# Maxima of a head group: one long spreading copy by ScalarE, or a short one and a spread by VectorE

## The chip, the cores and the metric
The kernel runs on one core of a Trainium2 chip. The metric is the device time of one execution in microseconds (us), as the median of several runs. The engines are TensorE (PE, its weight loads PEld), VectorE (DVE), ScalarE (ACT), GpSimd (POOL) and SyncE (SP, which issues the DMAs). Each runs its own instructions in order, and they wait for one another by semaphores.

## The reference, cut to what matters
Two layers, each a gated attention and a gated block of attention with a mixture of experts, over 16 sequences of 256 tokens with 256 channels, 16 heads of 16 channels:

```
x = x + tanh(g_xattn[0]) * xattn0(ctx, layernorm(x), ...)     # stage 0: keys and values from ctx, key bias and mask
x = x + tanh(g_ffn[0])   * ffn0(layernorm(x), ...)            # stage 1: self attention + top-2 of 8 linear experts
x = x + tanh(g_xattn[1]) * xattn1(layernorm(x), ctx, ...)     # stage 2: 512 keys, half of them from ctx
x = x + tanh(g_ffn[1])   * ffn1(layernorm(x), ...)            # stage 3: causal attention, then top-2 of 8 GELU experts
attn = softmax(q k^T + bias);  out = attn v                   # in each stage, for each head
```

What matters here is the softmax: for each query and head the maximum of its 256 (in stage 2, 512) scores is subtracted before the exponential.

## The kernel before, in words
The attention part takes the four stages u = 0 to 3 one after another, and in each the 16 sequences b; a pair (u, b) is a job. In a job each head h goes through these steps:

- `S`: TensorE multiplies queries by keys into one of two PSUM banks `s_ps` (L870 to L876). VectorE takes the row maxima into `mx` (L1112; in stage 3 with the causal mask, L1105) and gives the bank back (`s_read`).
- `M`: once for each group of HG = 8 heads (two groups a job), GpSimd negates the 8 maxima of every query and splits each into three bf16 parts (L1043 to L1050), in `mp` [128 queries, 27 columns] for each half of the tokens: 3 columns of ones and 3 x 8 parts.
- `MT`: TensorE transposes `mp` into rows 96 to 122 of `tr_ps` (L883), 27 rows of 256 queries. ScalarE copies these rows into rows 96 to 122 of `qs`, the stacked query operand, once for each of the 8 heads of the group: one ACTIVATE whose input is read 8 times (L989). It gives `tr_ps` back (`tr_read`).
- `T`: TensorE multiplies keys by queries, transposed, into one of two banks `t_ps`; the 27 extra rows of `ks` and `qs` add the bias and subtract the maximum (L901, in stage 3 L897 and L898). The first T of a group waits for MT's copy. ScalarE takes the exponential into `ex` (L995) and gives the bank back (`t_read`). In stage 3 GpSimd clears the future keys (L1035).
- `PV`: after four heads TensorE multiplies by the values (L926) and ScalarE copies the result out (`ot`, L999). `OT`: TensorE transposes it into `tr_ps` (L937), the same bank that MT uses, and VectorE divides by the sums (L1119, L1121) and gives the bank back, also by `tr_read`.

Around them are layer norms (`LNS`, `LNP`, `LNX`; L1077, L1014, L1090), projections `Q`, `K`, `V`, `PROJ`, their split into bf16 parts on GpSimd (L1026 to L1030), DMAs that stack the parts as rows, in stage 1 the experts (L847, L1176), and `FIN` (L1197) or `PROJ`, which end a job.

The order of the instructions on each engine is not written by hand. `orders()` is a planner that runs when the kernel is built: a list scheduler over all steps of all jobs, with a cost in microseconds for each step and engine (`STAGES`), a hop between engines (`HOPS`), and the rules of the banks. Each engine then issues its instructions in the order found, and the `*_AT` tables turn the order into semaphore counts. So a changed cost in `STAGES` can move any step in any queue of the attention part.

```
"M": [("pool", 1.3)], "MT": [("pe", 0.12), ("act", 1.86)],
act.wait_ge(tr_ready, TR_AT[step] + 1)
act.activation(qs[q_at][PRODUCTS:ROWS, k * HG:(k + 1) * HG, :],
               tr_b[PRODUCTS:ROWS, 0:T].unsqueeze(1).broadcast_to([ROWS - PRODUCTS, HG, T]), ACT.Copy).then_inc(tr_read, 1)
```

Behind the attention part (from about 1920 us) come routing, the experts of the last stage and their combination, each a part of its own.

Of the kernel before, what the change touches and what calls it, by code (L numbers as in the profile page):

```python
# [7 lines left out]
BF16 = mybir.dt.bfloat16  # L8
# [3 lines left out]
ACT = mybir.ActivationFunctionType  # L12
# [3 lines left out]
B, T, D = 16, 256, 256  # L16
# [13 lines left out]
HG = H // G  # L30
# [8 lines left out]
PRODUCTS = 6 * HD  # L39
# [21 lines left out]
def kv_at(u, b, src=0):  # L61
# [14 lines left out]
    "UNBIAS": [("dve", 1.8)], "BPROJ": [("pool", 1.27)],  # L76
    "GATE": [("pe", 0.9), ("dve", 0.65)], "GEXP": [("act", 0.22)], "TOP": [("dve", 0.6)],
# [3 lines left out]
    "OTT": [("pe", 0.44), ("act", 0.6)], "PROJ": [("pe", 0.87), ("pe", 0.87), ("dve", 0.75)], "FIN": [("dve", 0.86)],  # L81
    "STOREX": [("sp", 0.5), ("wire", 7.5)]}
# [228 lines left out]
def counted(steps):  # L311
    return {s: n for n, s in enumerate(steps)}


def of_kind(engine, *names):
    return [s for s in dict.fromkeys(ORDER[engine]) if s[0] in names]
# [9 lines left out]
TR_AT = counted(of_kind("pe", "MT", "OT"))  # L326
PRE_AT = counted(of_kind("pe", *PRE))
M_AT = counted(of_kind("pool", "M"))
KSPLIT_AT = counted(of_kind("pool", "KSPLIT"))
QSPLIT_AT = counted(of_kind("pool", "QSPLIT"))  # L330
VC_AT = counted(of_kind("pool", "VC"))
# [141 lines left out]
def attention_phase(nc, a):  # L473
# [3 lines left out]
    with own:  # L477
# [20 lines left out]
        qs = ring("qs", NQ, [ROWS, H, T], BF16); ks = ring("ks", NKV, [ROWS, H, T], BF16)  # L498
        va = ring("va", NKV, [P, NT, H, VW])
        mx = ring("mx", NQ, [P, H, 2])  # L500
        mr = ring("mr", 2, [P, NT, HG]); mp = ring("mp", 4, [P, NT, ROWS - PRODUCTS], BF16)
        ex = sb("ex", [P, EXPS, 2 * T])
        ot = ring("ot", 2, [P, T])
# [29 lines left out]
        xn_ready, vc_ready, bproj_added, moments, rooted = sem("xn_ready"), sem("vc_ready"), sem("bproj_added"), sem("moments"), sem("rooted")  # L533
        s_ready, s_read, t_ready, t_read = sem("s_ready"), sem("s_read"), sem("t_ready"), sem("t_read")
        m_ready, tr_ready, tr_read, pv_ready, pv_read = sem("m_ready"), sem("tr_ready"), sem("tr_read"), sem("pv_ready"), sem("pv_read")
        past_kept = sem("past_kept")
        lg_ready, lg_exp, top_done, fin_done = sem("lg_ready"), sem("lg_exp"), sem("top_done"), sem("fin_done")
        dve_step, pool_step = sem("dve_step"), sem("pool_step")

# [139 lines left out]
        with nc.Block() as block:  # L679
# [93 lines left out]
            def _(pe):  # L773
# [29 lines left out]
                for step in ORDER["pe"]:  # L803
# [74 lines left out]
                    elif name == "MT":  # L878
                        pe.wait_ge(m_ready, M_AT[("M", u, b, k)] + 1)
                        if TR_AT[step]:  # L880
                            pe.wait_ge(tr_read, TR_AT[step])
                        for t in range(NT):
                            last = pe.transpose(tr_b[PRODUCTS:ROWS, t * P:(t + 1) * P], mp[(2 * j + k) % 4][:, t, :], ident_b[:, :])  # L883
                        last.then_inc(tr_ready, 1)
                    elif name == "T":
                        n = T_AT[step]
                        h, src = k
                        if step == T_FIRST[(u, b, h // HG)]:
                            pe.wait_ge(tr_read, TR_AT[("MT", u, b, h // HG)] + 1)
                        if n >= 2:  # L890
                            pe.wait_ge(t_read, n - 1)
                        at = kv_at(u, b, src)
                        if u == 1 and b < NKV and step == T_FIRST[(u, b, h // HG)]:
                            pe.wait_ge(bias_set, UNBIAS_AT[("UNBIAS", u, b, 0)] + 2)
                        dst, key = t_ps[n % 2], ks[at % NKV]
                        if u == 3:
                            pe.matmul(dst[:, 0:T], key[0:ROWS, h, 0:P], qs[q_at][0:ROWS, h, :], start=True, stop=True)  # L897
                            last = pe.matmul(dst[:, T:T + P], key[0:ROWS, h, P:T], qs[q_at][0:ROWS, h, P:T], start=True, stop=True)  # L898
                        else:
                            for t in range(NT):  # L900
                                last = pe.matmul(dst[:, t * T:(t + 1) * T], key[0:ROWS, h, t * P:(t + 1) * P],  # L901
                                                 qs[q_at][0:ROWS, h, :], start=True, stop=True)
                        last.then_inc(t_ready, 1)
                    elif name == "PV":
                        v = PV_AT[step]
                        srcs = sources(u)
                        slots = {(i, r): T_AT[("T", u, b, (k * QH + i, r))] for i in range(QH) for r in range(srcs)}
                        if u == 3:
                            pe.wait_ge(past_kept, max(PAST_AT[("T", u, b, (k * QH + i, 0))] for i in range(QH)) + 1)
                        else:  # L910
                            pe.wait_ge(t_read, max(slots.values()) + 1)
                        if u == 0:
                            pe.wait_ge(vc_ready, VC_AT[("VC", u, b, 0)] + 1)
                        else:
                            wait_copied(pe, ("V", u, b, 0))
                        if u == 2:
                            pe.wait_ge(vc_loaded[b % 2], 16 * (b // 2 + 1))
                        if v:
                            pe.wait_ge(pv_read, v)
                        for r in range(srcs) if turns(step) == 1 else (turn,):  # L920
                            val = va[kv_at(u, b, r) % NKV]
                            for t in range(NT):
                                q0 = P if u == 3 and t == 1 else 0
                                for i in range(QH):
                                    e = ex[:, slots[(i, r)] % EXPS, t * T:t * T + T - q0]
                                    last = pe.matmul(pv_ps[i * VW:(i + 1) * VW, q0:T], val[:, t, k * QH + i, :], e,  # L926
                                                     start=r == 0 and t == 0, stop=r == srcs - 1 and t == NT - 1,
                                                     tile_position=(0, i * VW))
                        if ends:
                            last.then_inc(pv_ready, 1)  # L930
                    elif name == "OT":
                        v = PV_AT[("PV", u, b, k)]
                        pe.wait_ge(pv_read, v + 1)
                        if TR_AT[step]:
                            pe.wait_ge(tr_read, TR_AT[step])
                        for t in range(NT):
                            last = pe.transpose(tr_ps[:, t * P:(t + 1) * P], ot[v % 2][:, t * P:(t + 1) * P], ident[:, :])  # L937
                        last.then_inc(tr_ready, 1)

            @block.scalar  # L940
            def _(act):
                for step in ORDER["act"]:
# [35 lines left out]
                    elif name == "V":  # L978
                        wait_values_free(act, u, b, sources(u) - 1)
                        dst = va[kv_at(u, b, sources(u) - 1) % NKV]  # L980
                        end_pre(act.activation(dst[:, :, :, 0:HD], bank[:, :].rearrange("p (t h d) -> p t h d", t=NT, h=H), ACT.Copy))
                    elif name == "CT":
                        end_pre(act.activation(combt[j % 2][:, :], bank[0:E, 0:T], ACT.Copy))
                    elif name == "GEXP":
                        act.wait_ge(lg_ready, LG_AT[("GATE", u, b, 0)] + 1)
                        act.activation(flat(pr[j % 2]), flat(lg[j % 2]), ACT.Exp).then_inc(lg_exp, 1)
                    elif name == "MT":
                        act.wait_ge(tr_ready, TR_AT[step] + 1)
                        act.activation(qs[q_at][PRODUCTS:ROWS, k * HG:(k + 1) * HG, :],  # L989
                                       tr_b[PRODUCTS:ROWS, 0:T].unsqueeze(1).broadcast_to([ROWS - PRODUCTS, HG, T]), ACT.Copy).then_inc(tr_read, 1)  # L990
                    elif name == "T":
                        n = T_AT[step]
                        act.wait_ge(t_ready, n + 1)
                        w = 3 * P if u == 3 else 2 * T
                        act.activation(ex[:, n % EXPS, 0:w], t_ps[n % 2][:, 0:w], ACT.Exp).then_inc(t_read, 1)  # L995
                    elif name == "PV":
                        v = PV_AT[step]
                        act.wait_ge(pv_ready, v + 1)
                        act.activation(ot[v % 2][:, :], pv_ps[:, 0:T], ACT.Copy).then_inc(pv_read, 1)  # L999
# [56 lines left out]
            def _(dve):  # L1056
# [7 lines left out]
                for step in ORDER["dve"]:  # L1064
# [33 lines left out]
                    elif name == "S":  # L1098
# [11 lines left out]
                        else:  # L1110
                            dst = mx[q_at][:, h, src:src + 1] if u == 2 else mx[q_at][:, h, :]
                            dve.tensor_reduce(dst, s_ps[n % S_BANKS][:, :].rearrange("p (a b) -> p a b", a=dst.shape[-1]), AX.X, ALU.max).then_inc(s_read, 1)  # L1112
                    elif name == "OT":
                        v = PV_AT[("PV", u, b, k)]
                        dve.wait_ge(tr_ready, TR_AT[step] + 1)
# [745 lines left out]
```

## Time and profile before

| | us |
|---|---|
| three runs | 2731.59, 2734.83, 2737.47 (median 2734.83) |
| the profiled run | 2733.68 |
| its span from first to last instruction | 2732.0 |
| TensorE busy in the span | 2326.2 (85%) |
| VectorE | 1705.4 (62%) |
| ScalarE | 1381.1 (51%) |
| GpSimd | 917.7 (34%) |

A row of a group of instructions reads: line, engine, operation, output <- input by the program's names, out <- in (partitions x elements, type), xcount | busy us, mean ns of one | idle time of the engine just before them, and what ended it. Matmuls are pipelined and their ends are modelled, so a busy TensorE isn't one at its peak. Waits name who came last.

### The profile page before, as it was taken

The page shows a single profiled execution, that of the slowest core. Times are in us where ns is not written, and L with a number is a line of the kernel's source. Part 1 is how long each engine was busy: PE and PEld are TensorE (multiplying, and loading weights), DVE is VectorE, ACT ScalarE, POOL GpSimd, SP SyncE. Part 2 cuts the span into 40 slices and gives each one's busy share as a digit, 9 for nine tenths or more (in the row PEclk, how much of TensorE's full clock was granted, in tenths as well). Part 3 has the DMA queues.
Part 4 walks back from the last instruction along what each step waited for, and adds up shares of the span by engine and source line. Part 5 has one row for each costly group of instructions (what it writes and reads, how often), then busy time and mean ns, then how long its engine had stood idle before and what let it go on. Part 6 is the DMA issues. An engine that isn't in the chain of part 4 may idle for free. (4 is left out here: it accounts for less than half of the span.)

```text
span 2732.0 us, 52598 instructions
## 1 busy us (share of the span) xinstructions
PE 2326.2 (85%) x17492; PEld 1615.3 (59%) x17493; DVE 1705.4 (62%) x4564; ACT 1381.1 (51%) x2430; POOL 917.7 (34%) x1769
## 2 busy tenths in 40 slices
PE   3889899999999999999999999898337999999920
PEld 1445555455555555666566666665337999999920
DVE  4668796766776766766766667665455434344358
ACT  3779863454444447777777777676110222222211
POOL 5355322131232152233322257665001333333321
PEclk9989999999999999999999999999556999999965
DMA  7888633242332354454454446553560111111144
GB/s 227 215 210 209 150 97 78 51 96 55 81 82 76 94 126 117 118 122 117 113 126 118 104 110 140 133 129 76 204 189 12 35 36 36 35 35 34 36 148 167
DMA packets 214243, 296.34 MB, mean 108 GB/s; under 512 B 33109, under 2 KB 152703, under 8 KB 207776
## 3 DMA queue, kind: packets, MB, share of 16 engines
q1 hardware_dynamic: 183808, 253.78, 36.5%
q10 hardware_dynamic: 23328, 22.06, 2.6%
q0 software_dynamic: 6912, 17.97, 2.1%
q8 instruction: 115, 1.88, 0.3%
q14 instruction: 80, 0.66, 0.1%
HBM read 201.41 MB, written 93.22 MB: 108 GB/s over the span
## 5 line engine op out<-in xcount | busy, mean ns | idle before, releaser
L1112 DVE TENSOR_REDUCE mx<-s_ps 128x2 f32<-128x512 f32 (+1 forms) x1024 | 657.2, 683 | 217.5 <-PE s_ps L870 141.3
L995 ACT ACTIVATE ex<-t_ps 128x512 f32<-128x512 f32 (+1 forms) x1280 | 683.8, 577 | 191.7 <-PE t_ps L901 146.9
L901 PE MATMUL t_ps<-qs,ks 123*128 123x256 bf16 x2048 | 362.1, 278 | 10.3 <-ACT ex L995 6.5
L926 PE MATMUL pv_ps<-ex,va 128*32 128x256 f32 (+1 forms) x5120 | 324.7, 380 | 2.5 <-POOL ex L1035 2.5
L989 ACT ACTIVATE qs<-tr_ps 27x2048 bf16<-27x2048 bf16 x128 | 239.4, 1870 | 146.5 <-PE tr_ps L883 143.8
L847 PE MATMUL pre_ps<-wexp,xt 128*128 128x512 f32 x512 | 264.5, 625 | 6.8 <-DVE moe L1176 2.6
L1631 PEld LDWEIGHTS x_up_ps<-x_rows_t,x_wnow 128*128 128x128 f32 x2272 | 266.4, 193 | 5.3 <-issue 0.9
L1631 PE MATMUL x_up_ps<-x_rows_t,x_wnow 128*128 128x128 f32 x2272 | 267.0, 276 | 1.1 <-DVE x_pre L1694 0.7
L901 PEld LDWEIGHTS t_ps<-qs,ks 123*128 123x128 bf16 x2048 | 175.0, 99 | 143.4 <-ACT ex L995 66.2
L1641 PE MATMUL x_y_ps<-wdn,x_act 128*128 x1136 | 257.1, 379 | 0.7 <-DVE x_y L1702 0.7
L1661 ACT ACTIVATE x_rows_t<-x_rt_ps 128x256 f32<-128x256 f32 x72 | 27.7, 384 | 439.8 <-PE x_rt_ps L1620 439.8
L1641 PEld LDWEIGHTS x_y_ps<-wdn,x_act 128*128 128x128 f32 x1136 | 210.3, 190 | 26.8 <-issue 1.1
L876 PE MATMUL s_ps<-ks,qs 99*128 99x256 bf16 (+1 forms) x1024 | 190.3, 286 | 36.5 <-DVE mx L1112 25.1
L926 PEld LDWEIGHTS pv_ps<-ex,va 128*32 128x32 f32 x5120 | 142.2, 111 | 131.6 <-issue 49.9
L1105 DVE CUSTOM_DVE_ANT_0 s_ps<-s_ps,late 128x128 f32<-128x128 f32 (+1 forms) x512 | 166.6, 388 | 64.1 <-PE s_ps L873 63.7
L1043 POOL TENSOR_SCALAR mp<-mx 128x16 bf16<-128x16 f32 x128 | 34.8, 272 | 505.2 <-DVE mx L1112 473.6
L870 PE MATMUL s_ps<-ks,qs 96*128 96x256 bf16 x1024 | 185.1, 275 | 21.3 <-DVE mx L1112 16.0
L1689 DVE COPY x_wnow<-wup 128x1024 f32 x144 | 98.8, 688 | 141.8 <-PE x_up_ps L1631 135.4
L876 PEld LDWEIGHTS s_ps<-ks,qs 99*128 99x128 bf16 (+1 forms) x1024 | 89.0, 101 | 139.3 <-DVE mx L1112 75.2
L999 ACT ACTIVATE ot<-pv_ps 128x256 f32<-128x256 f32 x256 | 99.0, 387 | 142.6 <-PE pv_ps L926 140.1
L1176 DVE SCALAR_TENSOR_TENSOR moe<-pre_ps,comb,moe 128x256 f32<-128x256 f32 x256 | 123.1, 481 | 61.6 <-PE pre_ps L847 55.3
L1026 POOL TENSOR_TENSOR ak<-ak,pk 128x512 f32<-128x512 f32 x64 | 74.1, 1158 | 232.5 <-ACT pk L976 135.3
(254 smaller groups left out, 3764.1 us busy)
## 6 DMA issues: line engine op xcount, KB each, us to landing
q_parts<-pq SPq DMA_DIRECT2D x128, 192.0 KB
qs<-q_parts SPq DMA_DIRECT2D x64, 384.0 KB, 5.0
qs<-q_parts SPq DMA_DIRECT2D x192, 128.0 KB, 5.8
k_parts<-pk SPq DMA_DIRECT2D x96, 192.0 KB
ks<-k_parts SPq DMA_DIRECT2D x96, 192.0 KB
ks<-k_parts SPq DMA_DIRECT2D x288, 64.0 KB
ks<-ctx_k_parts SPq DMA_DIRECT2D x64, 192.0 KB
ks<-ctx_k_parts SPq DMA_DIRECT2D x192, 64.0 KB
```

The costliest lines, as they stand in the source:

```text
L847: end_pre(step, pe.matmul(bank[:, :], xt_now[:, turn, t * P:(t + 1) * P], wexp[:, turn, e:e + 2, :].rearrange("p e n -> p (e n)"), start=t ...
L870: last = pe.matmul(dst[:, r * T:(r + 1) * T], q(src), key(r)[0:rows, h, :], start=True, stop=True)
L876: last = pe.matmul(dst[:, t * T:(t + 1) * T], q(t), key(0)[0:rows, h, :], start=True, stop=True)
L901: last = pe.matmul(dst[:, t * T:(t + 1) * T], key[0:ROWS, h, t * P:(t + 1) * P], qs[q_at][0:ROWS, h, :], start=True, stop=True)
L926: last = pe.matmul(pv_ps[i * VW:(i + 1) * VW, q0:T], val[:, t, k * QH + i, :], e, start=r == 0 and t == 0, stop=r == srcs - 1 and t == NT - 1,
L989: act.activation(qs[q_at][PRODUCTS:ROWS, k * HG:(k + 1) * HG, :], tr_b[PRODUCTS:ROWS, 0:T].unsqueeze(1).broadcast_to([ROWS - PRODUCTS, HG, ...
L995: act.activation(ex[:, n % EXPS, 0:w], t_ps[n % 2][:, 0:w], ACT.Exp).then_inc(t_read, 1)
L1105: last = dve.tensor_tensor_reduce(out=seen, in0=seen, in1=late[:, 2 * P - w:2 * P], scale=1.0, scalar=FUTURE, op0=ALU.add, op1=ALU.max, ac ...
L1112: dve.tensor_reduce(dst, s_ps[n % S_BANKS][:, :].rearrange("p (a b) -> p a b", a=dst.shape[-1]), AX.X, ALU.max).then_inc(s_read, 1)
L1176: last = dve.scalar_tensor_tensor(out=moe[r][:, t, :], in0=bank[:, n * D:(n + 1) * D], scalar=comb[r][:, t, e + n:e + n + 1], in1=moe[r][: ...
L1631: last = pe.matmul(up_ps[h][:, g * P:(g + 1) * P], wnow[k][h][:, c, g * P:(g + 1) * P], rows_t[:, c, :], start=c == 0, stop=c == DC - 1)
L1641: last = pe.matmul(y_ps[:, 0:D], act_t[k][h][:, g, :], wdn[:, bass.ds(x, 1), f, :].rearrange("p e n -> p (e n)"), start=f == 0, stop=f == ...
```

## The change
The group's rows are copied out of PSUM once, by ScalarE, into a new SBUF tile `ms` (two buffers, 256 bf16 a row). VectorE then copies them from there under the eight heads in `qs`, reading the 256 elements 8 times. The first T of a group waits for VectorE's copy, by a new semaphore `m_spread`; ScalarE waits, before it writes a buffer of `ms`, for the spread that read it last. `tr_ps` is free after ScalarE's copy. The planner's `MT` gets the cost 0.39 on ScalarE and a new third part of 0.75 on VectorE in place of 1.86 on ScalarE.

```diff
-    "S": [("pe", 0.222), ("dve", 0.68)], "M": [("pool", 1.3)], "MT": [("pe", 0.12), ("act", 1.86)],
+    "S": [("pe", 0.222), ("dve", 0.68)], "M": [("pool", 1.3)], "MT": [("pe", 0.12), ("act", 0.39), ("dve", 0.75)],
...
+MT_AT = counted(of_kind("act", "MT"))
+SPREAD_AT = counted(of_kind("dve", "MT"))
+assert SPREAD_AT == MT_AT
...
+        ms = ring("ms", 2, [ROWS, T], BF16)
...
-                            pe.wait_ge(tr_read, TR_AT[("MT", u, b, h // HG)] + 1)
+                            pe.wait_ge(m_spread, SPREAD_AT[("MT", u, b, h // HG)] + 1)
...
                     elif name == "MT":
+                        at = MT_AT[step]
                         act.wait_ge(tr_ready, TR_AT[step] + 1)
-                        act.activation(qs[q_at][PRODUCTS:ROWS, k * HG:(k + 1) * HG, :],
-                                       tr_b[PRODUCTS:ROWS, 0:T].unsqueeze(1).broadcast_to([ROWS - PRODUCTS, HG, T]), ACT.Copy).then_inc(tr_read, 1)
+                        if at >= 2:
+                            act.wait_ge(m_spread, at - 1)
+                        act.activation(ms[at % 2][PRODUCTS:ROWS, :], tr_b[PRODUCTS:ROWS, 0:T], ACT.Copy).then_inc(tr_read, 1)
...
+                    elif name == "MT":
+                        dve.wait_ge(tr_read, TR_AT[step] + 1)
+                        dve.tensor_copy(qs[q_at][PRODUCTS:ROWS, k * HG:(k + 1) * HG, :],
+                                        ms[MT_AT[step] % 2][PRODUCTS:ROWS, :].unsqueeze(1).broadcast_to([ROWS - PRODUCTS, HG, T])).then_inc(m_spread, 1)
```

## Rows read from the trace of the kernel before

**Rows 1.** Stretches: us, busy time of each engine, PEclk, DMA share, GB/s
```profile
67.00:385.00 318.00, 279.13 (x2447) 159.86 (x2446) 243.55 (x532) 255.88 (x426) 141.25 (x284) 0.94 0.74 187
385.00:1010.00 625.00, 589.31 (x3402) 329.82 (x3401) 433.39 (x1073) 283.35 (x519) 155.98 (x297) 0.96 0.32 79
1010.00:1590.00 580.00, 551.63 (x5049) 357.56 (x5051) 397.94 (x872) 434.78 (x742) 171.67 (x330) 1.00 0.49 116
1590.00:1920.00 330.00, 296.37 (x2656) 201.17 (x2646) 208.99 (x1106) 229.72 (x428) 210.09 (x486) 0.96 0.50 117
```

**Rows 2.** The page's costliest groups of instructions, whole span
```profile
L1112 DVE TENSOR_REDUCE mx<-s_ps 128x2 f32<-128x512 f32 (+1 forms) x1024 | 657.2, 683 | 217.5 <-PE s_ps L870 141.3
L995 ACT ACTIVATE ex<-t_ps 128x512 f32<-128x512 f32 (+1 forms) x1280 | 683.8, 577 | 191.7 <-PE t_ps L901 146.9
...
L989 ACT ACTIVATE qs<-tr_ps 27x2048 bf16<-27x2048 bf16 x128 | 239.4, 1870 | 146.5 <-PE tr_ps L883 143.8
...
L1689 DVE COPY x_wnow<-wup 128x1024 f32 x144 | 98.8, 688 | 141.8 <-PE x_up_ps L1631 135.4
...
L999 ACT ACTIVATE ot<-pv_ps 128x256 f32<-128x256 f32 x256 | 99.0, 387 | 142.6 <-PE pv_ps L926 140.1
```

**Rows 3.** Waits of TensorE's weight loads in stage 0: us, times, longest
```profile
PEld s_ps L876 <- DVE mx L1112: 45.7, 88, 3.8
PEld t_ps L901 <- ACT ex L995: 26.2, 63, 1.1
```

**Rows 4.** The same waits in stage 1
```profile
PEld s_ps L876 <- DVE mx L1112: 23.6, 60, 1.1
PEld t_ps L901 <- ACT ex L995: 21.6, 59, 0.7
PEld pre_ps L847 <- DVE moe L1176: 16.8, 33, 1.7
```

**Rows 5.** The same waits in stage 2
```profile
PEld s_ps L870 <- DVE mx L1112: 62.9, 157, 2.8
PEld t_ps L901 <- ACT ex L995: 18.4, 75, 0.7
```

**Rows 6.** The same waits in stage 3
```profile
PEld s_ps L872 <- DVE mx L1105: 27.9, 70, 1.0
PEld t_ps L897 <- ACT ex L995: 13.7, 35, 2.5
```

**Rows 7.** Timeline in stage 2: start us, us, engine, instruction [idle before <-releaser]
```profile
1205.79 0.39 PE L901 MATMUL t_ps<-qs,ks 123*128 123x256 bf16 x2
...
1206.08 1.87 ACT L989 ACTIVATE qs<-tr_ps 27x2048 bf16<-27x2048 bf16 x1
...
1207.19 0.39 PE L870 MATMUL s_ps<-ks,qs 96*128 96x256 bf16 x2 [0.57 <-DVE mx L1112]
...
1207.79 0.39 PE L870 MATMUL s_ps<-ks,qs 96*128 96x256 bf16 x2 [0.21 <-DVE mx L1112]
...
1208.72 0.38 PE L901 MATMUL t_ps<-qs,ks 123*128 123x256 bf16 x2
```

**Rows 8.** Line L989, who waited for it: us, times
```profile
  PE tr_ps L937: 7.7, 13
```

**Rows 9.** VectorE's groups in stage 0
```profile
L1090 DVE TENSOR_SCALAR xn<-xs,mv,rstd 128x256 f32<-128x256 f32 x30 | 13.4, 486 | 0.0
...
L1077 DVE BATCH_NORM_STATS2 stats<-xs 128x6 f32<-128x256 f32 x28 | 10.4, 413 | 9.2 <-DMA xs<-in_x 9.2
```

**Rows 10.** VectorE's groups in stage 2
```profile
L1090 DVE TENSOR_SCALAR xn<-xs,mv,rstd 128x256 f32<-128x256 f32 x24 | 8.7, 403 | 0.0
```

**Rows 11.** VectorE's groups in stage 3
```profile
L1090 DVE TENSOR_SCALAR xs<-xs,mv,rstd 128x256 f32<-128x256 f32 x24 | 14.4, 639 | 3.4 <-POOL rstd L1014 3.3
```

**Rows 12.** Timeline in stage 0
```profile
222.17 0.28 PE L883 MATMUL tr_ps<-ident_b,mp 128*27 128x128 bf16 x2
...
224.84 1.87 ACT L989 ACTIVATE qs<-tr_ps 27x2048 bf16<-27x2048 bf16 x1
```

More of the change, by code:

```diff
@@ L535, in attention_phase @@
         m_ready, tr_ready, tr_read, pv_ready, pv_read = sem("m_ready"), sem("tr_ready"), sem("tr_read"), sem("pv_ready"), sem("pv_read")
-        past_kept = sem("past_kept")
+        past_kept, m_spread = sem("past_kept"), sem("m_spread")
         lg_ready, lg_exp, top_done, fin_done = sem("lg_ready"), sem("lg_exp"), sem("top_done"), sem("fin_done")
```

## The prediction

> **What bounds the kernel now.** I read the stretches first [rows 1]. The change touches the attention part alone, which ends near 1920 us; the 812 us behind it stay. That part has four stages of 16 jobs: 67 to 385, 385 to 1010, 1010 to 1590 and 1590 to 1920 us. TensorE is busy for 88 to 95% of each, VectorE for 77, 69, 69 and 63%, ScalarE for 80, 45, 75 and 70%. TensorE's clock is granted at 0.94 to 1.00, so next to nothing is to be had there. A busy TensorE isn't a full one: its records include latency and the waits of single matmuls don't show in the share. So I read next what a step costs [rows 2], then who keeps TensorE waiting, stage by stage [rows 3 to 6].
>
> In every stage the largest named wait of the weight loads is that of the scores S for a free bank, which VectorE's row maxima (L1112, in the last stage L1105) give back: 45.7, 23.6, 62.9 and 27.9 us, and in stage 1 the expert sums add 16.8. Together 176.9 us. The wait of the transposed scores T for a free bank, which ScalarE's exponentials (L995) give back, is 26.2, 21.6, 18.4 and 13.7 us, together 79.9. So VectorE is waited for twice as much as ScalarE, although in stages 0 and 2 ScalarE is the busier of the two. The change takes work from the one that is waited for less and gives some to the other; whether it pays is a matter of sizes.
>
> ScalarE's long copy (L989, 1870 ns, 128 times, 239.4 us) [rows 2] is three times as long as anything else that it does in this part. What such a block does can be seen in stage 2 [rows 7]: TensorE's last T matmul ahead of it starts at 1205.79, the copy takes ScalarE from 1206.08, both T banks are full, and the next T matmul starts at 1208.72. TensorE has only S left to do and runs against VectorE: idle for 0.57, 0.21 and 0.20 us, 0.98 in all (three such gaps, the first two are shown). The view puts that down to VectorE, but a free T bank would have filled it. Of the 31 copies in the steady part of this stage ten have such a gap of 0.82 to 0.98 us; all 31 gaps add up to 10.3 us.
>
> **What goes: ScalarE.** The copy shrinks from 2048 to 256 elements a partition, PSUM to SBUF. The nearest row is the copy of pv_ps (L999), 256 elements, 387 ns [rows 2]; no row is further from it than the 577 ns of an exponential. So 128 x (1.870 - 0.387) = 189.8 us leave ScalarE, 15.8% of the 1203.7 us that it is busy in the four stages. What that gives back: (a) the same share of the 79.9 us of waits for exponentials, 12.6 us; (b) half of the ten large gaps of the kind of [rows 7], 10 x 0.93 / 2 = 4.6 us, half since S is then still there to be done; (c) tr_ps is one bank for the maxima and for the outputs' transposes, and is given back after the short copy: TensorE waited 7.7 us for that [rows 8], of which 1.483 of 1.870, so 6.1 us, go. Relief 23 us. Its lower end is (a) alone, its upper end all gaps of stage 2 and twice (a), 42 us.
>
> **What comes: VectorE.** 128 copies of 27 x 2048 bf16 within SBUF. No row of the kernel before shows a bf16 copy on VectorE, so I bound one. The only copy within SBUF in the trace is L1689: 128 x 1024 f32, 4096 bytes a partition, 688 ns [rows 2]; the new one moves 4096 bytes a partition too: 0.69 us if bytes count. If elements count at that copy's pace, with the fixed part taken from the 413 ns of a 256-element BATCH_NORM_STATS against the 683 ns of a 512-element reduction (1.055 ns an element, 143 ns fixed) [rows 2, 9], it is 143 + 2048 x (688 - 143) / 1024 = 1233 ns; at the reduction's pace 143 + 2048 x 1.055 = 2304 ns. I take 0.69, by the row that is the same operation. That is 88 us, 6.9% of VectorE's 1283.9 busy us in the four stages, and the same share of the 176.9 us of waits is 12.2 us. Ends: nothing (it lands in VectorE's own 69 to 77%) and 24 us (each added microsecond twice as harmful as the average one); below nothing it can't be, since nothing is taken from VectorE.
> The Trainium skill's page "VectorE: DVE Perf Modes", section "The perf-mode tier table", gives 693 ns for a bf16 copy of 2048 elements within SBUF, and about 1224 and 2293 ns for the slower modes; by it the sum would be the same. No row here shows the bf16 case.
>
> **GpSimd beside it.** VectorE's normalising step (L1090) is the same 256-element instruction in every stage: 403 ns on average in stage 2, 486 in stage 0 and 639 in stage 3 [rows 9 to 11]. GpSimd is busy 30% of stage 2, but 44% of stage 0 and 64% of stage 3 [rows 1]: where GpSimd is at work, VectorE's instruction from SBUF to SBUF is held up. I give each spread the same extra: 32 x 0.083 + 32 x 0.236 = 10 us of VectorE, by the ratio 12.2 / 88 worth 1.4 us.
> The rule behind it is in the Trainium skill, "SBUF — State Buffer", section "Who interferes with whom": a copy in a two-port mode and a GpSimd instruction shut each other out for a whole instruction. The three means agree with it; that the new copy takes part in it no row shows. If it holds, GpSimd is delayed as well, by up to 0.69 us a spread; GpSimd is idle enough to take that.
>
> **The new waits.** VectorE now waits for tr_read, ScalarE's short copy. Behind the waiting spread stand the reductions, which free TensorE's S banks, and FIN. In stage 0 the short copy can stand behind exponentials: TensorE's transpose of the maxima ends at 222.45 and the copy starts at 224.84 [rows 12], 2.4 us later. The planner will put the spread where it expects the copy to be done; where it is late, all of VectorE is late. I take 0.1 us for each of the 32 in stage 0, 3 us, ends 0 and 10. ScalarE's wait for the spread before the last (ms has two buffers) and for the group's spread on TensorE's side cost nothing: the chain tr_ps, ms, qs is 0.39 + 0.69 us and two hops, not 1.87. The shorter chain is worth about 0.5 us at the start and at the end, 1 us.
> The planner lays out all engines' instructions anew with the new costs. That can't be read from the trace. The irregular loads in stage 0 may fall better or worse; I allow 10 us to either side.
>
> **Sum.** 23 + 1 given back, 12.2 + 1.4 + 3 taken: about 8 us gained. The profiled run took 2733.7 us, 1.7 of them outside its span of 2732.0; it lies 1.1 us below the median of 2734.8. So the profiled run becomes about 2726, the median 2727.
>
> **The rivals.**
> (1) Forecast: ScalarE's relief is worth more than VectorE's load. 2727, its own range 2714 to 2729. For it: the copy is ScalarE's longest block and two T banks can't bridge it [rows 7]. Against it: ScalarE isn't what is mostly waited for. Chance 0.45; 0.04 more for stronger relief at the upper end, near 2710.
> (2) What one gives the other takes: (a) alone, 12.6 us, against 12.2 and 1.4. The time stays at 2730 to 2740. Chance 0.24.
> (3) Slower: VectorE takes over as the limit. In stage 0 it has 243.6 us of work in 318, the spreads and their delays make 268, more than the 255.9 that ScalarE has now; in stages 2 and 3 the S banks already wait for it most. Where TensorE has two S steps out and nothing else ready, each spread delays it by its whole length. It decides once over a third of the 96 spreads of stages 0, 2 and 3 do so: all of them cost 66 us, two thirds 44, less the relief of 23: 2756; half of them, 2744. For it: the S waits of [rows 3, 5]. Against it: VectorE has 23 to 37% of each stage free. Chance 0.21.
> (4) The change doesn't do what it says: the spread runs at elements' pace. 158 us at 1233 ns are 12% of VectorE's load and cost 22 us by the same ratio, 295 us at 2304 ns at least 41: 2735 to 2755. Chance 0.06.
>
> **How the numbers follow.** The bound of what a measurement can tell from no change is 0.2%, 5.5 us: 2729.4 to 2740.3. Faster 0.49 (case 1); same 0.24 (case 2); slower 0.27 (cases 3 and 4). The range leaves out the ends of cases 1 and 3: 2706 to 2752.
>
> **What would show it.** ACT's copy at 0.38 us and DVE's at 0.69; if it is 1.2 or 2.3, case 4. ScalarE's busy time in 67 to 1920 us down by 190, VectorE's up by 90 to 100. TensorE's waits for exponentials below 70 us in total, those for maxima at about 190; if these rise above 210, case 3. The wait of the outputs' transposes for the maxima's copy nearly gone. L1090 unchanged. I'd be wrong above all if the new order moved a load or a projection so that a stage gained or lost tens of microseconds for reasons of its own.

## The result: 26 us slower

| | us, median | against before |
|---|---|---|
| before | 2735.3 | |
| changed | 2760.7 (2758.4 to 2765.9) | 1.0097, 95% interval 1.0079 to 1.0115 |
| forecast | 2727 (2706 to 2752) | |

The difference of 25.5 us is clear of the noise. The profiled run has a span of 2759.8 us where the kernel before had 2732.0. Stretches of the changed kernel, as [rows 1] (us, busy PE, PEld, DVE, ACT, POOL, clock, DMA share, GB/s):

```profile
67.00:385.00 318.00, 266.18 (x2328) 152.32 (x2332) 257.39 (x523) 202.47 (x409) 143.86 (x277) 0.92 0.70 179
...
1010.00:1590.00 580.00, 560.08 (x5009) 357.02 (x5007) 421.97 (x833) 381.84 (x736) 174.85 (x320) 1.00 0.48 120
```

These bounds are those of the old stages, of which stages 0 and 2 are shown. ScalarE's share has fallen and VectorE's risen as meant; TensorE gets through fewer matmuls in the first stretch (2328 for 2447). By the start of each stage's last closing step (FIN, or PROJ in stages 2 and 3) the timelines say where the time went:

| closing step of the stage's last job, starts at us | stage 0 | 1 | 2 | 3 | from there to the end |
|---|---|---|---|---|---|
| before | 381.8 | 1010.5 | 1589.2 | 1918.8 | 813 |
| changed | 394.7 | 1030.3 | 1614.4 | 1945.3 | 814 |
| lag added in the stage | 12.9 | 6.9 | 5.4 | 1.3 | |

Stage 0 is the worst; it is the stage where VectorE and ScalarE were both fullest (77 and 80% busy). In stage 2 ten jobs in a row take 35.0 us each, where the old pattern of 36.7, 39.2 and 29.7 has a mean of 35.2: there the time is lost only at the edges.

The two copies themselves are what was forecast. Durations (min/median/max, ns) of VectorE's spread and ScalarE's short copy:

```profile
L1121 DVE COPY qs<-ms x128: 690/691/1565, 68.9 to 1930.3; 27x2048 bf16<-27x2048 bf16 x128
...
L996 ACT ACTIVATE ms<-tr_ps x128: 376/376/377, 68.5 to 1929.9; 27x256 bf16<-27x256 bf16 x128
```

TensorE's weight loads wait as follows over the whole span, in place of [rows 3 to 6] (the kernel before had 75.2, 64.5 and 34.1 us in the three S groups):

```profile
PEld t_ps L905 <- ACT ex L1001: 73.8, 208, 1.2
PEld s_ps L880 <- DVE mx L1118: 73.4, 170, 3.7
PEld s_ps L874 <- DVE mx L1118: 63.3, 191, 0.8
...
PEld s_ps L876 <- DVE mx L1111: 37.6, 92, 1.6
...
PEld t_ps L905 <- DVE qs L1121: 34.2, 33, 3.5
```

The S waits add up to 174.3 us, before to 173.8: no change. The waits for exponentials are no smaller either (83.6 with stage 3's line, before 79.9). What is new is the wait of the first T for the spread, 39.7 us with stage 3's. One in stage 0:

```profile
229.54 0.38 ACT L996 ACTIVATE ms<-tr_ps 27x256 bf16<-27x256 bf16 x1
...
231.08 1.50 DVE L1207 SCALAR_TENSOR_TENSOR xs<-o,tanh_g,xs 128x512 f32<-128x512 f32 x1
...
231.97 1.07 POOL L1025 COPY va<-ctx 128x512 f32<-128x512 f32 x1
...
232.60 0.99 DVE L1121 COPY qs<-ms 27x2048 bf16<-27x2048 bf16 x1
...
233.65 1.03 PE L905 MATMUL t_ps<-qs,ks 123*128 123x256 bf16 x4 [3.18 <-DVE qs L1121]
```

The rows are in `ms` at 229.92. VectorE has the output division and FIN ahead of the spread in its queue; FIN takes 1.50 us beside GpSimd's instructions where 0.75 is its median, the spread 0.99, and TensorE stands still for 3.18 us. So the copied maxima reach `qs` 4.0 us after the short copy began, where one long copy took 1.87.

### The profile page after: what moved, and what is told of

The parts are those of the page before. It is cut to its first block and busy times, and to the rows that moved or that the text cites. A ratio compares the mean times of both kernels' runs of the same rounds, so it can differ in the third digit from the quotient of the medians.

```text
span 2759.8 us, 52852 instructions
## 1 busy us (share of the span) xinstructions
PE 2337.4 (85%) x17492; PEld 1609.3 (58%) x17493; DVE 1811.8 (66%) x4692; ACT 1196.6 (43%) x2430; POOL 928.8 (34%) x1769
## 5 line engine op out<-in xcount | busy, mean ns | idle before, releaser
L905 PE MATMUL t_ps<-qs,ks 123*128 123x256 bf16 x2048 | 368.0, 283 | 35.3 <-DVE qs L1121 22.9
L905 PEld LDWEIGHTS t_ps<-qs,ks 123*128 123x128 bf16 x2048 | 174.3, 100 | 185.5 <-ACT ex L1001 73.8
L851 PE MATMUL pre_ps<-wexp,xt 128*128 128x512 f32 x512 | 255.1, 606 | 12.7 <-DVE moe L1186 8.2
L880 PE MATMUL s_ps<-ks,qs 99*128 99x256 bf16 (+1 forms) x1024 | 201.0, 293 | 33.9 <-DVE mx L1118 23.8
L795 PE MATMUL pre_ps<-xt,w 128*128 128x256 f32 x512 | 140.6, 403 | 5.6 <-DVE va L1102 1.8
```

The source lines that it names most:

```text
L795: last = pe.matmul(dst[:, half * T:(half + 1) * T], w[:, c, at + half * P:at + (half + 1) * P], src[:, c, :], start=c == 0, stop=c == DC - 1)
L851: end_pre(step, pe.matmul(bank[:, :], xt_now[:, turn, t * P:(t + 1) * P], wexp[:, turn, e:e + 2, :].rearrange("p e n -> p (e n)"), start=t ...
L880: last = pe.matmul(dst[:, t * T:(t + 1) * T], q(t), key(0)[0:rows, h, :], start=True, stop=True)
```

## Experiments: what a spread costs, and what the relief is worth

Each was timed against the kernel before on the same chip. Its medians were 2732 to 2737 from one set of runs to the next, so a few microseconds between runs of different sets mean nothing. Behind each time stand, in brackets, its ratio to the kernel before of the same set and the 95% interval of the ratio.

**The order of one, the copy of the other.** The changed order with ScalarE's long copy:

```diff
-pe.wait_ge(m_spread, SPREAD_AT[("MT", u, b, h // HG)] + 1)
+pe.wait_ge(tr_read, TR_AT[("MT", u, b, h // HG)] + 1)
-act.activation(ms[at % 2][PRODUCTS:ROWS, :], tr_b[PRODUCTS:ROWS, 0:T], ACT.Copy)   # and VectorE's spread
+act.activation(qs[...8 heads...], tr_b[...].broadcast_to(...), ACT.Copy)
```

> Three theories for the 25 us lost. ORDER: the planner's new order of all steps is worse in itself, whoever makes the copy. QUEUE: the first T of a group waits for a spread that stands behind reductions in VectorE's queue. LOAD: VectorE's additional 98 us of work make TensorE wait for its S banks. This kernel keeps the changed kernel's order and gives ScalarE the whole copy of 1870 ns again (no spread, nothing on VectorE). ORDER expects it as slow as the changed kernel or slower, 2755 to 2785, since its order counts on a short copy. QUEUE and LOAD expect most of the loss gone: 2735 to 2745.

Measured 2875.9 (1.0525, 1.049 to 1.056), far above both ranges. And the old order with the split copy, the spreads put into VectorE's queue by the times of the old plan:

```diff
-"MT": [("pe", 0.12), ("act", 0.39), ("dve", 0.75)]
+"MT": [("pe", 0.12), ("act", 1.86)]
+    keyed.append((BEGUN[(s, 1)] + 0.49, -1, s))     # the spread's place in VectorE's order
```

> The order of the kernel before on every engine, but the copy split as in the change, with each spread put into VectorE's order at the time at which the old plan has ScalarE's copy 0.49 us under way. ORDER expects this to be at least as fast as the kernel before, 2715 to 2735, since ScalarE is relieved and the order is the good one. QUEUE expects about 2735 to 2745, since the spread stands early in VectorE's order here. LOAD expects 2750 to 2765, as the work on VectorE is the same as in the change.

Measured 2811.6 (1.0301, 1.026 to 1.034), worse than any theory said. An order holds only for the costs that it was made with; swapping one part alone doesn't split the loss. Only runs that differ in one thing inside the same order, or that are each planned for their own work, can be compared.

**The relief alone.** ScalarE copies under the first head only, VectorE does nothing: in the old order, then planned anew with 0.39, and later with 0.40 as a second order.

```diff
-act.activation(qs[q_at][PRODUCTS:ROWS, k * HG:(k + 1) * HG, :], tr_b[...].unsqueeze(1).broadcast_to([ROWS - PRODUCTS, HG, T]), ACT.Copy)
+act.activation(qs[q_at][PRODUCTS:ROWS, k * HG, :], tr_b[PRODUCTS:ROWS, 0:T], ACT.Copy)
```

> The same short copy without any spread (seven heads left out), but in the order of the kernel before on every engine. ScalarE gets 190 us of idle time and nothing else changes. If the relief of my sum is right, 2705 to 2720. If an order gives the time back only where it is planned for it, 2725 to 2733.

> What is ScalarE's relief worth at the most? The kernel before with the maxima copied once, 256 elements, straight under the first head of the group (the other seven heads don't get theirs: left out), nothing on VectorE, and planned anew with 0.39 us on ScalarE. LOAD, now: VectorE's spread costs more than the 14 us of my sum, and the relief of 23 us is real; then this kernel takes 2705 to 2715. FIT: the relief is worth little and the loss is that of a less lucky order; then it takes 2725 to 2740.

> The short copy under one head and no spread (seven heads left out), planned with 0.40 us instead of 0.39: another order for the same instructions. If the relief is what the first order showed, 2692 to 2708; if the first order was luck, 2710 to 2730.

Measured 2717.5 (0.9941, 0.992 to 0.996), 2699.1 (0.9887, 0.987 to 0.991) and 2691.1 (0.9842, 0.982 to 0.986). So 190 us off ScalarE are worth 18 us in the old order and 36 and 46 us (31 and 43 by the ratios) in an order made for it. The relief is real: near the 23 us of the sum in the old order, and larger where it was planned for.

**The spread alone, in one and the same order.** Both kernels of this pair have the old order with the spreads put in; one spreads under a single head.

```diff
-dve.tensor_copy(qs[q_at][PRODUCTS:ROWS, k * HG:(k + 1) * HG, :], ms[...].unsqueeze(1).broadcast_to([ROWS - PRODUCTS, HG, T]))
+dve.tensor_copy(qs[q_at][PRODUCTS:ROWS, k * HG, :], ms[MT_AT[step] % 2][PRODUCTS:ROWS, :])
```

> The old order with the spread put in (2811.6 us), but VectorE spreads under one head of eight, some 0.2 us instead of 0.69 (seven heads left out). The waits and the places are the same. LOAD expects 128 x 0.5 = 64 us less, most of the 79 us that the insertion cost: 2745 to 2755. If it is VectorE's standing still for ScalarE's copy, or its place in the order, that costs, the time stays above 2785.

Measured 2756.8 (1.0089, 1.007 to 1.011), 2 us above LOAD's range and 28 below the other theory's. So in the old order: no spread 2717.5, one head 2756.8, eight heads 2811.6. The last step is 54.8 us for 128 x 0.467 = 59.8 us of copying: over nine tenths of VectorE's added time becomes time of the kernel. The first step, 39.3 us for 128 copies of 0.223 us (28.5 us), is more than the copies' length; it also brings the new waits. A part of the reason is in VectorE's queue. Its timeline in the changed kernel:

```profile
1267.85 1.28 DVE L1118 TENSOR_REDUCE mx<-s_ps 128x1 f32<-128x512 f32 x2
1269.15 0.69 DVE L1121 COPY qs<-ms 27x2048 bf16<-27x2048 bf16 x1
1269.88 1.29 DVE L1118 TENSOR_REDUCE mx<-s_ps 128x1 f32<-128x512 f32 x2
```

Two reductions of 0.683 us take 1.28 together: they start 0.597 us apart and overlap. The spread overlaps with neither neighbour; it starts 0.02 to 0.03 us after the one ends and the next starts as long after it. From the second reduction (1268.45) to the third (1269.88) it is 1.43 us. The median of the 30 spreads that stand between two reductions is 1.434, 0.837 more than without a spread. By the same count in the changed order's one-head kernel (below), a copy that lasts 0.223 takes 0.370. The Trainium skill, page "VectorE: DVE Perf Modes", section "Two Vector instructions with no wait between them", says, as a model, that an instruction whose operands start in another group of 32 partitions than those before it is held until they have finished. The spread starts at partition 96, the reductions at 0, so the gaps agree. The semaphore waits are not what makes them: every reduction has one, also those that overlap, and in the kernel further below whose spreads wait for nobody (`e10_unwaited_spread`) none of the 64 spreads behind a reduction overlaps with it:

```profile
1322.08 0.69 DVE L1133 TENSOR_REDUCE mx<-s_ps 128x1 f32<-128x512 f32 x1 [2.75 <-PE s_ps L892]
1322.80 0.69 DVE L1135 COPY qs<-ms 27x2048 bf16<-27x2048 bf16 x1
1323.51 1.29 DVE L1133 TENSOR_REDUCE mx<-s_ps 128x1 f32<-128x512 f32 x2
```

Whether it is the start partition or something else about this copy, no run separates.

So a spread costs VectorE 0.837 us and not 0.69, an estimated 107 us for all 128, and with the delays by GpSimd (the 128 durations add up to 98.6 us instead of 88.3) some 117. TensorE's waits for VectorE in the old order show where it goes. Eight heads:

```profile
PEld s_ps L897 <- DVE mx L1135: 105.9, 188, 2.9
PEld s_ps L891 <- DVE mx L1135: 89.1, 183, 2.4
...
PEld s_ps L893 <- DVE mx L1128: 45.1, 87, 2.2
```

No spread:

```profile
PEld s_ps L876 <- DVE mx L1111: 82.4, 177, 3.9
PEld s_ps L870 <- DVE mx L1111: 68.4, 178, 2.3
...
PEld s_ps L872 <- DVE mx L1104: 37.2, 91, 1.0
```

240.1 us against 188.0: 52 more, of the 94 between the kernels. What the other 42 are, the lists of waits don't say.

**In the changed order.** The same shortening there:

> The changed kernel, its order and waits kept, but VectorE spreads the maxima under one head of eight only, 256 elements instead of 2048, some 0.2 us instead of 0.69 to 0.85 (the other seven heads don't get their maxima subtracted: left out). It takes about 65 us of VectorE's added 98 away. LOAD expects two thirds of the loss gone: about 2743. QUEUE expects the part that the spread's own length has in the wait gone, a quarter to a half of the loss, 2748 to 2755. ORDER expects it to change little, 2752 to 2760.

Measured 2750.9 (1.0075, 1.005 to 1.010), 9.8 us off 2760.7, or 6 by the ratios, whose intervals overlap: not the two thirds of LOAD, and within the range of QUEUE. This order was planned with 0.75 us for the spread; that it keeps that room free and can't use the gaps of a shorter one is a reading that no run tests.

**Is it the waiting or the work?** The T matmuls no longer wait for the spread; so that nothing is read before it is written, they use the 96 product rows only.

```diff
-if step == T_FIRST[(u, b, h // HG)]:
-    pe.wait_ge(m_spread, SPREAD_AT[("MT", u, b, h // HG)] + 1)
-pe.matmul(..., key[0:ROWS, h, ...], qs[q_at][0:ROWS, h, :], ...)
+pe.matmul(..., key[0:PRODUCTS, h, ...], qs[q_at][0:PRODUCTS, h, :], ...)
```

> The changed kernel with its order and all its copies, but the T matmuls use the 96 rows of the products alone and so wait for no maxima (left out: the subtraction of the maxima and the key bias). What is gone is TensorE's wait for the spread, 65.6 us by the list of waits of the changed kernel. QUEUE expects at least the 25 us back: 2725 to 2737. LOAD expects 2750 to 2758, since the reductions are delayed all the same. ORDER expects part of it back, 2740 to 2750.

Measured 2773.3 (1.0154, 1.013 to 1.018): slower than the change by 13 us, which no theory had. A control keeps the waits and changes the rows alone:

> The changed kernel with all its waits, but the T matmuls use the 96 product rows alone (left out: the subtraction of the maxima and the key bias). Against it the kernel without the wait (2773.3) differs in the wait alone. If the 96 rows cost 13 us or more, through the clock or otherwise, this takes 2775 to 2795 and the wait for the spread costs the difference, 5 to 20 us. If the rows cost nothing, it takes 2758 to 2764, and taking the wait away made the kernel slower in itself.

Measured 2789.1 (1.0186, 1.017 to 1.021). The 96 rows by themselves cost 28 us, and the wait for the spread is worth 2789.1 - 2773.3 = 15.8 us. The two come from different sets of runs; by the ratios it is 24 and 9 us, and the intervals of the second pair overlap. The lists of waits show why it is so little. With the wait, TensorE's weight loads wait 42.3 us for the spread and 165.9 for the S banks (64.7, 63.7 and 37.5 us); without it they wait 203.9 for the S banks (100.2, 63.9 and 39.8). Nine tenths of the wait come back as waits for VectorE's reductions. The stretch 67 to 1910 us in the change, in the control, and without the wait:

```profile
67.00:1910.00 1843.00, 1699.14 (x13276) 1025.96 (x13276) 1370.18 (x3612) 1000.19 (x2068) 673.95 (x1350) 0.97 0.47 116
```

```profile
67.00:1910.00 1843.00, 1705.44 (x13037) 1023.75 (x13040) 1355.43 (x3504) 988.14 (x2035) 657.58 (x1313) 0.95 0.47 114
```

```profile
67.00:1910.00 1843.00, 1702.73 (x13221) 1028.13 (x13220) 1363.79 (x3573) 1001.39 (x2064) 673.52 (x1345) 0.96 0.48 116
```

The granted clock is 0.97, 0.95 and 0.96: the kernels with 96 rows spend more time at the lower of the two levels (1.2 instead of 2.4 GHz). That goes with the 28 us; why the clock falls wasn't tried.

The work without any waiting, in the old order: the spreads copy a constant tile into the same rows, nobody waits for them and they wait for nobody.

```diff
-dve.wait_ge(tr_read, TR_AT[step] + 1)
-dve.tensor_copy(qs[...8 heads...], ms[MT_AT[step] % 2][...].broadcast_to(...))
+dve.tensor_copy(qs[...8 heads...], ms[0][...].broadcast_to(...))
```

> The kernel with the old order and the spread put in (2811.6 us), but nobody waits for the spread and it waits for nobody: VectorE spreads a constant tile into the same rows at the same places of its queue, ScalarE makes its short copy, the T matmuls wait for that copy and use the 96 product rows alone (left out: the subtraction of the maxima and the key bias). Against the same order without any spread (2717.5) it holds VectorE's bare time, 0.837 us for each of 128 from reduction to reduction. LOAD expects nearly the whole 94 us between the two, 2795 to 2812. CHAIN (T waits for ScalarE and then VectorE) expects at most half of it, below 2765.

Measured 2827.9 (1.0338, 1.032 to 1.036). It has the 96 rows too, whose price neither range contains; less the 28 us that these cost in the other order, 2800, which is 82 of the 94 us between no spread and eight heads. The correction is carried over from another order and so rough. But the S waits of this kernel need none: 105.7, 88.9 and 44.7, together 239.3 us, the 240.1 of the kernel with all its waits. So in the old order it is the work that costs, not the chain.

**How much is the luck of an order?** Only the planner's numbers differ in these. First the kernel before, 1.87 for 1.86:

> The kernel before with one number changed: the planner's cost of ScalarE's copy 1.87 instead of 1.86. It is the measured one, and the instructions are the same; 611 of ScalarE's steps and 1718 of TensorE's stand at another place of the order. It measures what a new order does by itself. FIT expects 10 to 30 us to one side or the other; LOAD expects it within 8 us of the kernel before, 2725 to 2741.

Measured 2732.4 (0.9984, 0.997 to 1.000): next to nothing, though it is one other order only. Then the changed kernel with 0.84 us for the spread, the time that it really takes:

```diff
-"MT": [("pe", 0.12), ("act", 0.39), ("dve", 0.75)]
+"MT": [("pe", 0.12), ("act", 0.39), ("dve", 0.84)]
```

> The changed kernel with the planner's cost of the spread at 0.84 us, what it takes of VectorE between two reductions, instead of 0.75. If a part of the loss is that the plan takes VectorE's step too short, 2740 to 2752; if the loss is VectorE's load itself, 2753 to 2765.

Measured 2736.5 (1.0004, 0.999 to 1.001): nearly all of the loss gone with the same instructions, and below both ranges. Whether it is the truer cost or luck, neighbours must tell:

> The changed kernel with the planner's cost of the spread at 0.74 us. COST: the same too short cost as in the change, so within 6 us of it, 2755 to 2767. LUCK: anywhere from 2730 to 2770, and not near its neighbour of 0.75.

> The changed kernel with the planner's cost of the spread at 0.76 us. COST: 2752 to 2765. LUCK: anywhere from 2730 to 2770.

> The changed kernel with the planner's cost of the spread at 0.83 us, close to the measured 0.837. COST: as with 0.84, 2731 to 2743. LUCK: anywhere from 2730 to 2770.

> The changed kernel with the planner's cost of the spread at 0.85 us. COST: as with 0.84, 2731 to 2743. LUCK: anywhere from 2730 to 2770.

| planned cost of the spread | 0.74 | 0.75 (the change) | 0.76 | 0.83 | 0.84 | 0.85 |
|---|---|---|---|---|---|---|
| us | 2770.1 | 2760.7 | 2760.9 | 2756.5 | 2736.5 | 2739.7 |

The three around the true cost have a mean of 2744, the three around 0.75 one of 2764: a truer cost seems to help. But 0.83 and 0.84 differ by 20 us, so single orders scatter by as much. COST missed at 0.74 (by 3 us) and at 0.83 (by 13), and LUCK, which expected anything from 2730 to 2770, can hardly miss. Six orders don't settle how the 20 us between the groups divide. What they do settle: over all six the mean is 2754.1, 19 us above the kernel before, and the best only equals it.

**Elsewhere than on VectorE.** The spread on GpSimd, in pairs of bf16 read as one f32:

```diff
-dve.tensor_copy(qs[...8 heads...], ms[...].broadcast_to([ROWS - PRODUCTS, HG, T]))
+pool.tensor_copy(qs[...8 heads...].bitcast(F32), ms[...].bitcast(F32).unsqueeze(1).broadcast_to([ROWS - PRODUCTS, HG, T // 2]))
```

> The change with the spread on GpSimd instead of VectorE, in f32 pairs (1024 elements, planned with 1.2 us), GpSimd waiting for its own last instruction before and after. LOAD expects that moving the work from VectorE, which the S banks wait for, gives most of the 62 us back: 2710 to 2735. If it is the additional step in the chain that costs, it is as slow as the change or slower: 2755 to 2790.

Measured 2738.8 (1.0019, 1.000 to 1.004), between the two ranges. With a copy of 1.034 us on GpSimd, longer than VectorE's and with the same additional step in the chain, the kernel is 15 us below the six orders' mean. It is one order, though, and two of the six were as fast, so this points towards VectorE's time as the cause but doesn't show it. And ScalarE alone, in pairs:

```diff
-"MT": [("pe", 0.12), ("act", 1.86)]
+"MT": [("pe", 0.12), ("act", 1.02)]
-act.activation(qs[...8 heads...], tr_b[PRODUCTS:ROWS, 0:T].unsqueeze(1).broadcast_to([ROWS - PRODUCTS, HG, T]), ACT.Copy)
+act.activation(qs[...8 heads...].bitcast(F32), tr_ps[PRODUCTS:ROWS, 0:T // 2].unsqueeze(1).broadcast_to([ROWS - PRODUCTS, HG, T // 2]), ACT.Copy)
```

> No VectorE at all: ScalarE copies under the eight heads as before, but reads and writes pairs of bf16 as one f32, 1024 elements instead of 2048; by the rows 0.16 us and 0.83 ns an element, 1.02 us instead of 1.87, and planned so. It takes 109 of the 190 us from ScalarE and adds nothing. If the relief is what the short copy alone showed (36 us for 190), about 21 us: 2705 to 2720. Should the f32 copy not be of full speed, 2735.

```profile
L989 ACT ACTIVATE qs<-tr_ps x128: 1016/1016/1019, 68.4 to 1878.0; 27x1024 f32<-27x1024 f32 x128
```

Measured 2711.5 (0.9909, 0.989 to 0.993). It takes 109 us off ScalarE, adds nothing to anyone, and beats both kernels: 22 us below the one before in the same set of runs, 49 below the changed one. That is one order too, but it lies 25 us below the best of the six.

## Why the prediction was wrong, step by step

- **Who is waited for** was read rightly: VectorE twice as much as ScalarE. The weight that this had was far too small.
- **The step that failed is "What comes: VectorE".** The copy's duration was right (0.69 forecast, 0.691 measured), two things after it were not. The queue loses 0.837 us a spread between two reductions, since the spread ends the overlap of its neighbours: 107 us, not 88. And the price of VectorE's time was taken as the share of the waits, 176.9 / 1283.9 = 0.14. Measured, it is 94 of 117 us in an order that wasn't made for it (0.80), and between the mean of the six planned orders and the mean of the two without a spread (2695.1) 59 of 117 us, 0.50. All that the spread brings was put at 12.2 + 1.4 + 3 = 16.6 us and is 59. A busy share of 63 to 77% looked like room. The likely reason that it wasn't: S has two banks, TensorE comes with bursts of S, and in a burst VectorE's added time is TensorE's own. The 52 us of new S waits in the old order speak for it; that this explains the whole price isn't shown.
- **The relief** had the right sign and, where it was planned for, half the size: 23 forecast; 18 in the old order, 36 and 46 in new ones. Its terms came out unevenly. The waits for exponentials fell by 13.7 us in the old order (66.2 for 79.9), close to the 12.6 of (a), but those for S rose by 14.2 (188.0 for 173.8) although the kernel is faster. In the two planned orders without a spread it is the other way round: 143.6 and 140.7 for S, 93.2 and 83.7 for exponentials. Of the 6.1 us of (c) the change got 3.9 (the wait for `tr_ps` fell from 7.7 to 3.8). Here too the share of waits was a poor price: waits move to whoever comes last.
- **The new wait** was put at 3 us and is worth 9 to 16, by the pair with 96 rows. The kind of case shown above had been described (short copy done, spread behind others in VectorE's queue), but priced at 0.1 us a time.
- **GpSimd beside it**: 10 us more of VectorE forecast, 98.6 - 88.3 = 10.3 measured. By stage the spreads last 0.809 us on average in stage 0, 0.707 in stage 2 and 0.849 in stage 3. So the total is in part luck: a spread was given 0.083 us more in stage 0 and 0.236 in stage 3, and got 0.119 and 0.159, with small extras in the other stages.
- **The planner** was allowed 10 us to either side. Six orders of the same instructions lie between 2736.5 and 2770.1, 17 to either side of their middle.
- **Rival 3** is what came, with its price (2756 for two thirds of the spreads in full) close to the mean of the orders. That closeness is luck: both of its terms were too small, 44 us for the spreads that cost 59, and 23 for a relief of 40. How many spreads delay TensorE by their whole length wasn't counted. Its mechanism fits what the old order showed, where it was tested; in the changed one the time shows as TensorE's wait for the spread instead of for S. So the sign that was named for it didn't come: the waits for maxima and expert sums were to rise above 210 us, and by the same lines they are 185, with the 39.7 for the spread 225. It got 0.21 where the argument for it, the S waits, was the strongest row of the profile. Rival 4 is out: the copy takes 0.691 us, as its bytes gave.

## What to carry to other kernels

Work moved to another engine must be priced by what that engine's queue loses, neighbours' overlap included, and if another engine waits for it in bursts, nearer to its full length (here 0.5 to 0.8 of it) than to its share of the waits (0.14). Before moving work, look whether it can be made smaller where it is: reading pairs of bf16 as f32 halved the copy's elements and won 22 us, where the move was meant to win 8. Where a planner orders the program, time several plans with costs beside the true one before a change is judged: here they spread by 34 us, more than the change itself.

## What the runs showed of the hardware beyond that

- Neighbouring reductions of VectorE (PSUM to SBUF, 0.683 us) start 0.597 us apart; a copy at partitions 96 to 122 between them adds 0.837 us if it lasts 0.690, and 0.370 if it lasts 0.223: 0.147 more than its length. The copy overlaps with neither neighbour, and it doesn't either where it waits for no semaphore.
- A bf16 copy of 27 x 2048 within SBUF, its source read eight times, takes VectorE 0.690 us, and GpSimd 1.034 as f32 pairs; ScalarE takes 1.870 from PSUM, and 1.016 as f32 pairs.
- T matmuls over 96 rows instead of 123, as many and as long, made the kernel 24 to 28 us slower with a granted clock of 0.912 for 0.925 over the profiled span. The cause is open.
